# Graph network kernel: one VectorE comparison of 2400 elements in place of two of 1200 in each batch of the adjacency build

## What is computed

```python
edge_index = jnp.stack([src, dst])
h = jnp.maximum(_layernorm(x, axis=-1), 0.0)
x = x + _L0_gnn_ref(h, edge_index, ...)
h = jnp.maximum(_layernorm(x, axis=-1), 0.0)
x = x + _L1_gnn_ref(h, edge_index, ...)

# in both: sums over the edges of a node, for instance
agg = jax.ops.segment_sum(xn[src], dst, num_segments=n)
agg = jax.ops.segment_sum(h[src] * norm[:, None], dst, num_segments=n)
```

## Time and profile before

| | |
|---|---|
| median of 3 runs | 1009.32 us (1008.55 to 1010.2) |
| the profiled execution | 1008.71 us |
| its span | 1006.9 us |
| busy TensorE, VectorE, ScalarE, GpSimd | 894.1, 579.8, 357.0, 66.0 us |
| mean granted TensorE clock | 0.975 |
| L1107 (keys, first two chunks) | 98 operations, 72.1 us, 775 ns each |
| L1089 (low parts) | 49 operations, 72.6 us, 1482 ns each |

### The profile page before, as it was taken

The page is one execution under the profiler, slowest core; times in us unless marked ns, Lnnn a source line. Parts: engine busy times, 40 slices in busy tenths (PEclk is TensorE's granted clock), DMA queues, the critical chain, the costliest instruction groups (busy, mean ns, idle before and its releaser), DMA issues.

```text
span 1006.9 us, 16997 instructions
## 1 busy us (share of the span) xinstructions
PE 894.1 (89%) x6863; PEld 585.9 (58%) x6863; DVE 579.8 (58%) x1570; ACT 357.0 (35%) x1041; POOL 66.0 (7%) x88
## 2 busy tenths in 40 slices
PE   2347999999999999999999999998987888899997
PEld 1245666766755557775575575567545545456555
DVE  5779999987937944463231148466362654616211
ACT  0777777751652001364011032367204412122100
POOL 4100000000000000000000000413002200220000
PEclk9969999999999999999999999999999698999999
DMA  5010000007930002003000001786015100241002
GB/s 161 9 29 2 1 2 1 3 1 298 402 118 1 1 1 66 1 1 131 1 1 1 1 2 48 268 227 194 15 44 167 45 1 1 67 194 69 1 1 66
DMA packets 39438, 66.48 MB, mean 66 GB/s; under 512 B 3525, under 2 KB 27310, under 8 KB 38838
## 3 DMA queue, kind: packets, MB, share of 16 engines
q1 hardware_dynamic: 34464, 45.94, 13.1%
q0 software_dynamic: 4000, 17.73, 5.3%
q10 hardware_dynamic: 886, 1.61, 0.5%
HBM read 28.96 MB, written 36.32 MB: 65 GB/s over the span
## 4 chain that ended last, share of the span: by engine, by line
PE 61%; DVE 25%; ACT 5%; DMA 3%; issue 2%; POOL 1%; ACTq 0%; DVEq 0%; SPq 0%; POOLq 0%
PE psum L3148 26%; PE psum L2643 7%; PE psum L2531 7%; DVE region L1107 6%; DVE region L1089 6%; PE psum L2872 4%; DVE region L1710 2%; PE psum L2608 2%; PE psum L2430 2%; PE psum L2994 2%; DVE region L1101 2%; POOL region L848 1%; PE psum L3096 1%; PE psum L2456 1%; DMA nodebuf<-in_x 1%
## 5 line engine op out<-in xcount | busy, mean ns | idle before, releaser
L3148 PE MATMUL psum<-adj,region 128*128 128x448 fp8e4 (+1 forms) x1200 | 202.6, 329 | 1.1 <-DVE region L1949 1.0
L3148 PEld LDWEIGHTS psum<-adj,region 128*128 128x128 f16 x1200 | 116.5, 98 | 81.0 <-DVE region L1949 1.7
L2089 ACT ACTIVATE adj<-psum 128x400 fp8e4<-128x400 f32 x196 | 98.0, 504 | 44.4 <-PE psum L2465 41.0
L2456 PE MATMUL psum<-region 128*128 128x150 bf16 x784 | 88.7, 239 | 27.3 <-DVE region L1107 18.8
L2456 PEld LDWEIGHTS psum<-region 128*128 128x128 bf16 x784 | 62.1, 102 | 62.5 <-DVE region L1107 34.0
L2430 PE MATMUL psum<-adj,region 128*128 128x448 fp8e4 x350 | 91.1, 352 | 0.0
L1977 DVE SCALAR_TENSOR_TENSOR region<-psum,unfit,region 128x448 f32<-128x448 f32 (+3 forms) x34 | 20.1, 622 | 110.6 <-PE psum L3148 98.4
L3148 PE MATMUL psum<-region 128*128 128x448 fp8e4 (+3 forms) x452 | 77.1, 330 | 3.3 <-DVE region L1949 3.3
L1710 DVE CAST region<-psum 128x512 fp8e4<-128x512 f32 (+2 forms) x87 | 46.6, 595 | 55.6 <-PE psum L2974 28.2
L1089 DVE TENSOR_TENSOR region<-iota_lo,region 128x2560 bf16<-128x2560 bf16 x49 | 72.6, 1482 | 5.5 <-PE psum L2465 5.2
L2243 ACT ACTIVATE region<-psum 128x512 fp8e4<-128x512 f32 (+6 forms) x109 | 58.7, 593 | 47.5 <-PE psum L3035 17.6
(11 more groups left out here) (388 smaller groups left out, 1341.2 us busy)
## 6 DMA issues: line engine op xcount, KB each, us to landing
both_table<-adj SPq DMA_DIRECT2D x1, 10000.0 KB, 28.8
adj_table<-adj SPq DMA_DIRECT2D x1, 10000.0 KB, 54.8
region<-dk_dram SPq DMA_DIRECT2D x2, 1568.0 KB, 7.1
both_table<-region SPq DMA_DIRECT2D x1, 2704.0 KB, 9.6
half_table<-region SPq DMA_DIRECT2D x2, 832.0 KB, 5.2
xs_dram<-nodebuf SPq DMA_DIRECT2D x1, 1600.0 KB, 5.2
nodebuf<-xs_dram SPq DMA_DIRECT2D x1, 1600.0 KB, 6.3
half_table<-region SPq DMA_DIRECT2D x2, 768.0 KB, 5.6
```

The costliest lines, as they stand in the source:

```text
L2089: nc.scalar.activation(adj_dests[:, :, 2 * WIN * q:2 * WIN * (q + 1)], psum[:, q % BUILD_BANKS, 0:2 * KEYS].rearrange("p (j t) -> p t j", ...
L2456: pe.matmul(bank[:, i * KEYS + k0:i * KEYS + k1], hot_lo[:, r, c * BATCH_PAIRS + j, :, i], hot_key[:, r, c, j, k0:k1, i], start=(c == 0 an ...
L3148: last = pe.matmul(psum[:, b if b < BLOCKS else LAST_BANK, 0:width], here[:, t, k, :], rows, start=(t == 0 and k == 0), stop=(t == n_src - ...
```

## The change

The keys of the second chunk are counted from the window's third destination (destination 2), so that they too run from 0 to 149. The first two chunks then compare with the same numbers, and one operation of 8 rows of 300 (2400 elements) replaces the two of 4 rows of 300. For that, `edge_keys` subtracts another base, `middle_base`, from slots 128 to 255, in three operations in place of one. The last batch still needs all 200 keys of the second chunk, which now run from -50 to 149: `iota_key` begins at -50 (`MIDDLE` = 50) and has 250 numbers, not 200, each twice. `hot_ready` counts three signals a batch, and TensorE reads the second chunk's one-hots 50 places further ahead. The row sums of ScalarE lie in one place (`lane_sums`, moved to another region), and the two operations on `early_sums` go.

```diff
-HOT_STEPS = 1 + CHUNKS
+HOT_STEPS = 3
+MIDDLE = CHUNK_DESTS[1][0] * TILES
...
-        iota_key = sb("iota_key", [P, KEYS, 2], BF16)
+        iota_key = sb("iota_key", [P, MIDDLE + KEYS, 2], BF16)
+        middle_base = sb("middle_base", [P, GROUPS], F32)
...
-        early_sums = sb("early_sums", [P, EARLY_SUMS], F32)
...
-        lane_sums = region1[:, 1430:1430 + PAIRS - EARLY_SUMS]
+        lane_sums = region3[:, HOT_COLS * P:HOT_COLS * P + PAIRS]
...
+        def keys_at(late):
+
+            return 0, 0 if late else MIDDLE
...
-            pool.iota(iota_key[:], pattern=[[1, KEYS], [0, 2]], base=0, channel_multiplier=0,
+            pool.iota(middle_base[:], pattern=[[P * WIN, GROUPS]], base=CHUNK_DESTS[1][0], channel_multiplier=WIN,
+                      allow_small_or_imprecise_dtypes=True).then_inc(consts_ready, 1)
+            pool.iota(iota_key[:], pattern=[[1, MIDDLE + KEYS], [0, 2]], base=-MIDDLE, channel_multiplier=0,
...
-                step(nc.vector.tensor_scalar(loc, dest, win_base[:, g:g + 1], None, ALU.subtract))
+                begin, middle, rest = slice(0, P), slice(P, 2 * P), slice(2 * P, SLOTS)
+                nc.vector.tensor_scalar(loc[:, begin], dest[:, begin], win_base[:, g:g + 1], None, ALU.subtract)
+                nc.vector.tensor_scalar(loc[:, middle], dest[:, middle], middle_base[:, g:g + 1], None, ALU.subtract)
+                step(nc.vector.tensor_scalar(loc[:, rest], dest[:, rest], win_base[:, g:g + 1], None, ALU.subtract))
...
-                for c in range(2):
-                    k0, k1 = hot_keys(late)[c]
-                    key_of = keys_of[:, c * BATCH_PAIRS:(c + 1) * BATCH_PAIRS]
-                    nc.vector.tensor_tensor(hot_key[:, r, c, :, k0:k1, :],
-                                            iota_key[:, k0:k1, :].rearrange("p (o n) i -> p o n i", o=1).broadcast_to((P, BATCH_PAIRS, k1 - k0, 2)),
-                                            key_of.broadcast_to((P, BATCH_PAIRS, k1 - k0, 2)),
+                if late:
+                    for c in range(2):
+                        k0, k1 = hot_keys(True)[c]
+                        i0 = MIDDLE if c == 0 else 0
+                        key_of = keys_of[:, c * BATCH_PAIRS:(c + 1) * BATCH_PAIRS]
+                        nc.vector.tensor_tensor(hot_key[:, r, c, :, 0:k1 - k0, :],
+                                                iota_key[:, i0:i0 + k1 - k0, :].rearrange("p (o n) i -> p o n i", o=1).broadcast_to((P, BATCH_PAIRS, k1 - k0, 2)),
+                                                key_of.broadcast_to((P, BATCH_PAIRS, k1 - k0, 2)),
+                                                ALU.is_equal).then_inc(hot_ready, 1)
+                else:
+                    n = 6 * TILES
+                    nc.vector.tensor_tensor(hot_key[:, r, 0:2, :, 0:n, :].rearrange("p c j n i -> p (c j) n i"),
+                                            iota_key[:, MIDDLE:MIDDLE + n, :].rearrange("p (o n) i -> p o n i", o=1).broadcast_to((P, 2 * BATCH_PAIRS, n, 2)),
+                                            keys_of[:, 0:2 * BATCH_PAIRS].broadcast_to((P, 2 * BATCH_PAIRS, n, 2)),
                                             ALU.is_equal).then_inc(hot_ready, 1)
...
-            step(nc.vector.tensor_reduce(search[:, 20:21], early_sums[:], AX.X, ALU.max))
-            step(nc.vector.tensor_scalar(search[:, 20:21], search[:, 20:21], MOST, None, ALU.is_gt))
             dve.wait_ge(bank_free, BUILD_BANKS + PAIRS)
             step(nc.vector.tensor_reduce(search[:, 17:18], lane_sums, AX.X, ALU.max))
-            nc.vector.scalar_tensor_tensor(search[:, 17:18], search[:, 17:18], MOST, search[:, 20:21], ALU.is_gt, ALU.max).then_inc(flag_sums_in, 1)
+            nc.vector.tensor_scalar(search[:, 17:18], search[:, 17:18], MOST, None, ALU.is_gt).then_inc(flag_sums_in, 1)
...
-                                     accum_out=early_sums[:, q:q + 1] if q < EARLY_SUMS else lane_sums[:, q - EARLY_SUMS:q - EARLY_SUMS + 1]
-                                     ).then_inc(bank_free, 1)
+                                     accum_out=lane_sums[:, q:q + 1]).then_inc(bank_free, 1)
...
-                    pe.wait_ge(hot_ready, HOT_STEPS * (b + 1) + (3 if b == BATCHES - 1 else 0))
+                    pe.wait_ge(hot_ready, HOT_STEPS * (b + 1) + (4 if b == BATCHES - 1 else 0))
...
-                                  hot_key[:, r, c, j, k0:k1, i], start=(c == 0 and i == 0), stop=False, skip_group_check=True)
+                                  hot_key[:, r, c, j, k0 - keys_at(b == BATCHES - 1)[c]:k1 - keys_at(b == BATCHES - 1)[c], i], start=(c == 0 and i == 0), stop=False, skip_group_check=True)
```

More of the change, by code:

```diff
@@ L72 @@
 SUMS_PER_PAIR = 2
-EARLY_SUMS = 32
 FITS = 7
@@ L1063, in edge_keys @@
                 nc.vector.tensor_copy(lo_rows[:, g, to_last], low[:, last])
-                step(nc.vector.tensor_scalar(loc, dest, win_base[:, g:g + 1], None, ALU.subtract))
+                begin, middle, rest = slice(0, P), slice(P, 2 * P), slice(2 * P, SLOTS)
+                nc.vector.tensor_scalar(loc[:, begin], dest[:, begin], win_base[:, g:g + 1], None, ALU.subtract)
+                nc.vector.tensor_scalar(loc[:, middle], dest[:, middle], middle_base[:, g:g + 1], None, ALU.subtract)
+                step(nc.vector.tensor_scalar(loc[:, rest], dest[:, rest], win_base[:, g:g + 1], None, ALU.subtract))
                 nc.vector.scalar_tensor_tensor(key_rows[:, g, whole], loc[:, whole], float(TILES), high[:, whole], ALU.mult, ALU.add)
                 nc.vector.scalar_tensor_tensor(key_rows[:, g, to_last], loc[:, last], float(TILES), high[:, last], ALU.mult, ALU.add).then_inc(keyed, 1)
-            dve.wait_ge(consts_ready, 10)
+            dve.wait_ge(consts_ready, 11)
             for g in range(GROUPS):
@@ L1097, in _ @@
                         for q in range(2):
-                            nc.vector.tensor_tensor(both_keys(r, q, True)[rows, w], iota_key[rows, :, :],
+                            nc.vector.tensor_tensor(both_keys(r, q, True)[rows, w], iota_key[rows, MIDDLE:MIDDLE + KEYS, :],
                                                     keys_of[rows, q2 + q].broadcast_to((64, KEYS, 2)), ALU.is_equal).then_inc(hot_ready, 1)
@@ L1118, in count_uncovered @@
                     keys_of = by_edge[:, 1, :, u0:u1]
-                    first = float(CHUNK_DESTS[c][0] * TILES)
+                    shift = MIDDLE if c == 1 else 0
+                    first = float(CHUNK_DESTS[c][0] * TILES - shift)
                     late_of, outside_of = (ap[:, 0:64 * n].rearrange("p (b w) -> p b w", w=n) for ap in (late, outside))
-                    step(nc.vector.tensor_scalar(late_of, keys_of, float(CHUNK_DESTS[c][1] * TILES), None, ALU.is_ge))
+                    step(nc.vector.tensor_scalar(late_of, keys_of, float(CHUNK_DESTS[c][1] * TILES - shift), None, ALU.is_ge))
                     step(nc.vector.scalar_tensor_tensor(outside_of, keys_of, first, late_of, ALU.is_lt, ALU.max, accum_out=uncovered[:, c:c + 1]))
@@ L1125, in count_uncovered @@
                         keys_of = by_edge[:, 1, last_batch, u2:u1]
-                        step(nc.vector.tensor_scalar(late[:, 0:u1 - u2], keys_of, 0.0, -1.0, ALU.is_ge, ALU.mult))
+                        step(nc.vector.tensor_scalar(late[:, 0:u1 - u2], keys_of, float(-shift), -1.0, ALU.is_ge, ALU.mult))
                         step(nc.vector.scalar_tensor_tensor(outside[:, 0:u1 - u2], keys_of, first, late[:, 0:u1 - u2], ALU.is_lt, ALU.mult,
@@ L2390, in _ @@
             last.then_inc(windows_counted, 1)
-            pe.wait_ge(consts_ready, 10)
+            pe.wait_ge(consts_ready, 11)
             pe.wait_ge(rows_known, 1)
```

## The result

| | time, median | runs | ratio to before (95%) |
|---|---|---|---|
| before | 1009.47 us | 6, 1008.55 to 1010.43 | |
| after | 1003.75 us | 6, 1001.55 to 1005.97 | 0.9945 (0.9929 to 0.996) |
| forecast | 1006.5 us (1004.8 to 1008.2) | | |

The profiled execution of after took 1003.48 us, its span is 1001.6 and the mean granted clock 0.978 (before 1008.71, 1006.9 and 0.975).

The account below looks back on a forecast made before the run. VectorE was taken to bound most of the adjacency build; 41 batches x 0.07 us = 2.87 us off the profiled 1008.71 us gives 1005.84, or 1006.5 us against the median, range 1004.8 to 1008.2 us.

Parts of the forecast that it names:

- The price of an instruction: Keys comparison on VectorE: one operation in place of two saves 0.07 us a batch, bounds 0 and 0.15 us.
- rival A: Keys comparison on VectorE: the fixed part is by the row or otherwise kept, nothing moves, 1009.3 us; chance 0.08.
- Rival B: Keys comparison on VectorE: an instruction costs its full 0.148 us, 6.1 us saved, 1003.2 us; chance 0.06.
- The count of 41: Adjacency build: of 48 savings, those of batches 2 to 37 and 43 to 47 reach the end, 2.87 us.
- The free edits: Extra base subtractions on VectorE (0.6 us taken) and GpSimd's longer iota_key (0.57 us) hide in idle time, at no cost.
- The flag: Tail of the flag: VectorE, two operations fewer, finishes some 0.4 us earlier, but TensorE comes later, so worth nothing.
- The scatter: Whole time: the runs' spread of about 0.8 us either way around 1006.5 us, after three runs of 1008.55 to 1010.2.
- rival C: TensorE loses its clock in batches with sums: three such batches lose 4.3 us, 1013.6 us; chance 0.05.
- The bounds of the cost itself: Adjacency build: 33 to 46 batches at 0.06 to 0.08 us each save 2.0 to 3.7 us.

Follow-up runs that it names:

- before made early: The kernel before with the subtraction ahead of batch 3 run over 2 of its 25 tiles, the rest zeroed earlier: 1005.93 us, ratio 0.9962.

## Why the prediction was right and wrong

**The price of an instruction: right.** 0.07 us by the starts was forecast; the batch went from 3.17 to 3.10, and with four operations to 3.31. The fixed part is paid by the instruction, not by the row of its pattern (8 rows of 300 now, 4 before), so rival A falls. Rival B falls too: the length of 1424 ns is again longer than the 1.32 us that the operation occupies. The Trainium skill (VectorE: DVE Perf Modes, The DRAIN you can't avoid) says that the next operation does not start until the pipe is empty, and then that one which is not held starts earlier. By the first half alone each removed instruction would give back 0.148 us, an estimate from the durations in the earlier trace rows; 0.07 was measured, and the trace agrees with the second half.

**The count of 41: right.** TensorE's first product of batch 38 tells what the batches up to 37 brought (timeline, TensorE, before and then after):

```profile
181.44 0.45 PE L2456 MATMUL psum<-region 128*128 128x150 bf16 x4
```

```profile
178.30 0.43 PE L2471 MATMUL psum<-region 128*128 128x150 bf16 x4
```

From the start of batch 2 on VectorE that is 120.87 and 118.35 us, 2.52 less: 36 x 0.07. From there to the start of batch 43 it is 13.13 and 13.08, nearly no gain, and from there to the last batch's first product 21.31 and 20.96, 5 x 0.07. Together that is the table's 2.92 us, 2.87 forecast. That batches 39 to 42 hide their share was shown from the other side when the norms were moved.

**The free edits: right.** GpSimd's numbers take longer and its wait for the edge table stays; the timeline of GpSimd in after, against the earlier trace rows:

```profile
3.75 0.16 POOL L813 IOTA middle_base<- 128x4 f32 x1
3.83 2.84 POOL L815 IOTA iota_key<- 128x500 bf16 x1
...
20.18 1.11 POOL L839 DMA_INDIRECT region<-edges,row_i  x1 [11.65 <-DMA edges<-region]
```

The keys of the last group and the squares' sum on VectorE, against the earlier trace rows:

```profile
38.26 0.28 DVE L1071 TENSOR_SCALAR region<-region,win_base 128x128 f32<-128x128 int32 x1
38.46 0.28 DVE L1072 TENSOR_SCALAR region<-region,middle_base 128x128 f32<-128x128 int32 x1
38.65 0.25 DVE L1073 TENSOR_SCALAR region<-region,win_base 128x64 f32<-128x64 int32 x1
...
43.04 3.49 DVE L1081 TENSOR_REDUCE tiny<-region 128x25 f32<-128x3200 f32 x1 [3.54 <-ACT region L2062]
```

A group's keys take 2.29 us where they took 2.02, so 4 x 0.27 = 1.1 us in all (0.6 was taken, too small a size but off the path; the bounds of 0.6 to 3.4 held). The idle time before the squares' sum went from 4.59 to 3.54 and still covers it. Undoing the merge alone, which leaves these edits in, gives 0.9999 (0.998 to 1.0017).

**The flag: right.** VectorE ends its last sum at 224.30 us, and its next operation waits 1.18 us for TensorE's product:

```profile
224.15 0.15 DVE L1243 TENSOR_SCALAR search<-search 128x1 f32<-128x1 f32 x1
225.47 0.16 DVE L1245 TENSOR_SCALAR search<-psum 128x1 f32<-128x1 f32 x1 [1.18 <-PE psum L2605]
```

**The scatter: wrong, and this is the step that failed.** The prediction's range took "the runs' spread of about 0.8 either way" from three runs. A hundred runs of before spread from 1004.66 to 1014.65 us with a standard deviation of 2.1, and a median of six is then off by about a microsecond (1.25 x 2.1 / 2.45 = 1.1), for either kernel. The bounds of the cost itself (2.0 to 3.7 us) held in the build's stretch (2.9); the error lay in the time around it.

**Where the scatter comes from** is shown in part. The prediction cites 0.50 and 0.68 us in the last batch as what the kernel does there ("The last batch is unchanged") and lets the clock enter as a loss alone (rival C). The profiles show that a low clock there is an event and not a part of each execution: to `flag` after took 13.52, 15.19 and 13.52 us, and before made early 13.52 and 15.20. Before lost time there in all three profiles, in two of them in the last batch itself and in one behind it. In later stages the time varies as well (the table's last column), by the clock and by other waits (`half_table` above). The whole time follows the clock: one straight line with a common slope through 231 timed runs of all kernels gives 0.57 us for each 0.001 of the mean granted clock, with 1.3 us of scatter left around it. Taken at a clock of 0.975, before is at 1008.6 us, the changed kernel at 1005.0 in its first six runs and 1005.3 in its second measurement, and after with two operations at 1008.5. At the same clock the merge is then worth 3.3 to 3.6 us (standard errors 0.4 and 0.6), near the 2.9 of the build's stretch. The first six runs had a mean clock of 0.9773 and the hundred of before 0.9740. The difference of 0.0033 makes 3.3 x 0.57 = 1.9 us, and with the merge's 3.3 us that is 5.2 of the 5.7 us that were seen.

How much of what goes beyond 2.9 us was luck is not settled. Over all 19 runs the changed kernel's mean lies 4.3 us below before's (standard error 0.6), 1.4 more than the build's stretch. Of that 0.8 goes with its higher mean clock (0.9754), and no run shows whether the change brings that clock or chance did.

**What would have been better.** The working of the build needed no other term. Three runs don't bound the scatter; a range of 2 us more to either side would have held the time. The forecast of 1006.5 us stands beside 1006.05 in the second measurement and a mean of 1004.85 over 19 runs.

## What to carry to other kernels

On an engine that is full, starts and not durations price an instruction that is merged away, and the price counts only in batches where that engine leads: here 0.07 us x 41 of 48. A stretch between two landmarks inside the trace measured the change to 0.02 us, where whole runs spread over some 10 us; read the effect there, and use the whole time to see what became of it. A low clock seen in one profile may be an event and not a part of the kernel: look at a second profile before it stands in a sum, or in a range.

## What the runs showed of the hardware

- The same pause of TensorE (2.14 to 2.17 us before the last batch) ended at the low level of the clock in 3 of the 16 profiles that have it (1.2 GHz, granted 0.50 over before's last batch) and at the full one in 13. All three have two operations.
- Behind a pause filled with idle products the next products ran at the full clock (1.00 over the last batch, 0.43 us for four products in batch 0), and a low clock came later (0.79 behind the last batch). No run shows that time was gained by it.
- TensorE busy without a gap lost its clock too: behind 28 single-column products it was granted 0.57 on average over 8 us.
- Back to back on VectorE, an operation of 2400 elements (1424 ns long) held the next one up for 1.32 us; two of 1200 in its place took 1.39, four of 600 took 1.52. The fixed part is 0.07 us for each, whatever the rows of the pattern.
